# Attention block: VectorE normalises the next sample's x at step 13 of each sample instead of step 14

## The reference

```python
x = _ln(src) * (1.0 + scale) + shift          # scale, shift from the timestep of the sample
q, k, v = (heads(x @ W + b) for W, b in ...)  # 16 heads of 16 features
scores = q @ k.T / 4 + attention_bias         # bias: 8 x 16 x 512 x 512, fp32
scores = where(src_mask, -inf, scores)
ctx = softmax(scores) @ v
x = x + (ctx @ Wo + bo)
return x + gelu2(_ln(x) * g2 + beta2 @ W1 + b1) @ W2 + b2
```

## Time and profile before

| | us |
|---|---|
| median of 3 runs | 982.52 |
| lowest, highest | 981.4, 982.77 |
| the profiled execution, its own time | 980.44 |
| its span, first to last instruction | 978.6 |
| attention part: samples 1 to 8 | up to about 650 |

### The profile page before, as it was taken

How to read it: one execution, slowest core, us unless ns; L and a number is a source line. 1 busy time by engine, 2 the same in 40 slices (tenths; PEclk the granted TensorE clock), 3 DMA queues, 4 the chain that set the end, 5 groups by cost and what they waited for, 6 DMA issues and landing times. The chain is left out here.

```text
span 978.6 us, 19957 instructions
## 1 busy us (share of the span) xinstructions
PE 926.8 (95%) x5758; PEld 614.0 (63%) x5838; DVE 737.4 (75%) x1991; ACT 670.3 (68%) x1118; POOL 708.5 (72%) x568
## 2 busy tenths in 40 slices
PE   5889999999999999999999999979899999999996
PEld 5656556656656655665665665545476777777574
DVE  8886887878879788788986978788345675668465
ACT  3576978898788787889878878878544453544333
POOL 1789789788878878978896897876454455558465
PEclk9999999999999999999999999999999999999998
DMA  8988988996997899799789889965211110111101
GB/s 301 337 312 280 375 326 273 341 392 228 329 390 288 288 379 349 247 341 390 248 310 391 291 290 373 367 228 172 84 44 44 44 44 24 42 66 44 44 22 65
DMA packets 127533, 229.96 MB, mean 235 GB/s; under 512 B 6512, under 2 KB 53872, under 8 KB 123632
## 3 DMA queue, kind: packets, MB, share of 16 engines
q1 hardware_dynamic: 127472, 229.26, 65.8%
HBM read 187.30 MB, written 41.94 MB: 234 GB/s over the span
## 5 line engine op out<-in xcount | busy, mean ns | idle before, releaser
L937 ACT ACTIVATE prob<-prob,nmax 128x512 f32<-128x512 f32 x512 | 357.9, 729 | 65.7 <-DVE nmax L760 62.5
L760 DVE CUSTOM_DVE_ANT_0 prob<-s_bank,big 128x512 f32<-128x512 f32 x512 | 339.0, 686 | 74.0 <-POOL big L1111 39.0
L591 PEld LDWEIGHTS t_bank<-ident,prob 128*128 128x128 f32 x2048 | 239.0, 141 | 163.7 <-issue 48.2
L591 PE MATMUL t_bank<-ident,prob 128*128 128x128 f32 x2048 | 317.0, 277 | 16.1 <-ACT prob L937 6.0
L1111 POOL TENSOR_TENSOR big<-big,mterm_early 128x2048 f32<-128x2048 f32 (+2 forms) x78 | 271.0, 3489 | 50.2 <-DMA big<-in_fside_Bx16xSxS 34.1
L944 ACT COPY pt<-t_bank 128x512 f32<-128x512 f32 x312 | 182.0, 587 | 42.4 <-PE t_bank L591 41.2
L579 PE MATMUL s_bank<-stack_k,stack_q 128*128 128x512 bf16 x432 | 165.1, 382 | 1.3 <-DVE nmax L760 0.7
L769 DVE COPY pt<-t_bank 128x512 f32<-128x512 f32 x200 | 137.5, 688 | 31.3 <-PE t_bank L591 30.9
L605 PE MATMUL o_bank<-pt,val 128*32 128x512 f32 x1024 | 123.2, 599 | 3.7 <-issue 1.0
L2209 POOL TENSOR_TENSOR gl<-big,gh 128x512 fp32r<-128x512 f32 x64 | 83.1, 1307 | 49.8 <-DVE gh L1751 49.8
L2060 ACT ACTIVATE big<-bank,late 128x512 f32<-128x512 f32 x62 | 42.6, 690 | 72.6 <-PE bank L1458 69.8
(11 more groups left out here) (248 smaller groups left out, 1460.4 us busy)
## 6 DMA issues: line engine op xcount, KB each, us to landing
big<-in_fside_Bx16xSxS SPq DMA_DIRECT2D x128, 1024.0 KB, 7.7
pieces_dram<-pieces SPq DMA_DIRECT2D x64, 384.0 KB, 6.9
stack_q<-pieces_dram SPq DMA_DIRECT2D x15, 1024.0 KB, 8.8
stack_k<-pieces_dram SPq DMA_DIRECT2D x15, 1024.0 KB, 9.9
pieces_dram<-pieces SPq DMA_DIRECT2D x32, 256.0 KB, 7.2
xin<-in_x SPq DMA_DIRECT2D x8, 512.0 KB, 8.7
x_dram<-x SPq DMA_DIRECT2D x8, 512.0 KB, 4.5
x1r<-x_dram SPq DMA_DIRECT2D x8, 512.0 KB, 4.6
```

Of the source, the lines that this page charges most:

```text
L591: last = pe.transpose(t_bank[n % 2][:, c * P:(c + 1) * P], prob[:, n % NT, c * P:(c + 1) * P], ident[:])
L760: dve.tensor_tensor_reduce(out=prob[:, n % NT, :], in0=s_bank[n % 3][:, :], in1=bias[:, h % NB, t, :], scale=-1.0, scalar=3e38, op0=ALU.ad ...
L937: act.activation(tile, tile, ACT.Exp, bias=nmax[:, n % NT:n % NT + 1], scale=-1.0).then_inc(exped.sem, 1)
```

## The change

The constant that says at which loop position VectorE normalises goes from 14 to 13. Nothing else changes: the same instructions, with the same waits, in another order on VectorE.

```diff
 HEADS_OF_LOADS = dict(x1=3, first=2, expert=4, W1=6, mask=5, store_0=7, store_1=11)
 STACK_0_AT, STACK_1_AT = (9, 10), (0, 1)
-STATISTICS_AT, DEVIATION_AT, NORMALISE_AT = 11, 12, 14
+STATISTICS_AT, DEVIATION_AT, NORMALISE_AT = 11, 12, 13
 WEIGH_AFTER = 17
```

## The result

The changed kernel takes 985.6 us (median of 22 executions) against 981.17 us before (22 executions). The ratio is 1.0039 with an interval of 1.0028 to 1.0051: 3.8 us slower (2.7 to 5.0). The forecast was +3.6 us and 986.1 us.

The account below looks back on a forecast made before the run. PE was taken to bound each sample, busy 78.80 of 80.45 us. 6 x 0.605 = 3.63 us for samples 2 to 7 plus 0 for the first, on the median 982.52, gave 986.1 us, range 982.7 to 987.4.

Parts of the forecast that it names:

- The normalise is asked for 0.6 us earlier and ends when it ended: Samples 2 to 7: GpSimd's mask addition of head 5 holds the normalise 0.91 us; it ends 1.04 us after that addition.
- The bias addition of step 16 comes behind it, 0.605 us: VectorE, samples 2 to 7: this addition, formerly free beside GpSimd's instruction, now follows the normalise and delays W half 1.
- Nothing of it is absorbed: Samples 2 to 7: the whole lateness passes into the time, 6 x 0.605 = 3.63 us, bounds 0 and 5.4 us.
- the longer wait for x: PE's wait before transposing x in samples 2 to 7 was to stay at 0.33 us.
- The new wait before that turn: PE, before the turn of step 16: a new wait of about 0.6 us, as copy 14 must first empty its bank.
- The first sample, taken as 0: First sample: normalise held to 52.47, ending at 53.51, PE's transposition 0.9 us earlier; net 0, ends -2.6 and +0.3 us.
- The case in which VectorE comes first: First sample: VectorE might get the shared ports first, delaying GpSimd's third piece and bias 16, so nothing is gained there.
- A: Rival: the 0.6 us on VectorE vanishes in PE's lead or GpSimd's next wait; 982.5 us, chance 0.11.
- B: Rival: mask addition ends before the normalise, which isn't held; PE gets x earlier, gain up to 2.9 us, 979.6; chance 0.07.
- C: Rival: mask addition ends some tenths earlier, or first sample's clock dip vanishes; +1.9 us, 984.4 us, chance 0.16.

Follow-up runs that it names:

- h5_two_13: Kernel before with GpSimd masking two of head 5's four tiles (PE adds the other two) and the normalise at position 13: 982.55 us, ratio 1.0017.
- the two probes: Kernel before plus one 128x32 VectorE instruction at position 13: a copy from SBUF 986.96 us (ratio 1.0074), a memset 981.54 us (1.0004).
- h5_two_14: Kernel before with GpSimd masking two of head 5's four tiles (PE adds the other two), the normalise staying at position 14: 982.89 us, ratio 1.0019.
- probe_memset: Kernel before plus one VectorE memset of a 128x32 tile at position 13, the normalise staying at 14: 981.54 us, ratio 1.0004.
- the delay: Kernel before plus three VectorE statistics of a constant tile between the normalise and W half 1, some 0.6 us a sample: 983.51 us, ratio 1.0026.

## Why the prediction was right, step by step

**The normalise is asked for 0.6 us earlier and ends when it ended.** Right, and shown: the distance from GpSimd's end is 1.04 us in all six samples of the changed kernel (1.05 and 1.03 where the rounded rows are subtracted). That GpSimd is the cause and not a coincidence of the trace is shown by h5_two_13 and by the two probes. The Trainium skill says so of the forms ("SBUF — State Buffer", section "Who interferes with whom": a tensor_scalar in a two-port mode contends with GpSimd, an instruction with at most one SBUF input outside these modes doesn't). The runs agree as far as they show: normalise and copy from SBUF are held, memset, statistics and bias addition are not; which mode an instruction ran in is in no row.

**The bias addition of step 16 comes behind it, 0.605 us.** Right: 307.74 to 308.35.

**Nothing of it is absorbed.** Right in substance: the timed price is 3.8 us, and 6 x 0.605 is 3.6. In the fourth sample PE's turn of step 16 moved by 0.47 us against PE's start on x, 0.6 forecast; the rest is in the longer wait for x, which was to stay at 0.33 and is 0.46. The new wait before that turn came, and for copy 14: the turn's weight load stood idle 0.61 us for it, 0.18 before, while the matmuls themselves stood idle 0.12 us.

The size is less sure than the near hit looks. In the profiled execution the end of the normalise falls behind by 0.65 to 1.06 us a sample from the second to the seventh, 0.88 in the mean and not 0.6, since the hold grew by more than the request moved: GpSimd's addition ended 0.99 to 1.60 us behind the request (1.24 in the mean), against 0.3 to 0.9 us behind the old one (0.50). That is 0.74 us more, where the forecast had 0.60. Its start is the landing of a load, which varied in the same way before. The forecast's time of 986.1 us owes its nearness to 985.6 also to luck: it was counted from the median of three executions, 982.52, and the kernel before came to 981.17 over 22, while the medians' difference came out 0.8 us above 3.6.

**The first sample, taken as 0.** It did not go as worked out. VectorE's first two instructions of the normalise, and GpSimd's second and third piece:

```profile
51.44 1.10 DVE L798 TENSOR_SCALAR xin<-xin,mv,rstd 128x256 f32<-128x256 f32 x1
52.47 1.24 DVE L798 TENSOR_SCALAR xin<-xin,mv,rstd 128x256 f32<-128x256 f32 x1
...
51.23 1.16 POOL L1108 TENSOR_TENSOR big<-big,mterm_early 128x512 f32<-128x512 f32 x1
52.35 1.20 POOL L1108 TENSOR_TENSOR big<-big,mterm_early 128x512 f32<-128x512 f32 x1
```

I had forecast one hold, by the third piece, and the end at 53.51. But the pieces lay 1 us later than before, because their load did (a wait of 5.58 us against 4.56; the first piece starts at 50.11 and not at 49.08, ahead of everything that the change touches), so that the request met the second piece. It was held twice: the first instruction got through at the border of two pieces, the next waited out the third piece. It ended at 54.27, PE began on x at 54.40 (before, 54.55), and the 3.4 us of granted clock 0.50 behind it stayed. The case in which VectorE comes first did not arise: both times GpSimd's piece had begun 0.1 to 0.2 us before. At the end of the second sample's normalise the changed kernel is 0.97 us behind. This 1 us is in the profiled execution's 5.7 us, of which 4.4 are from there to the seventh sample, and need not be in the median's. Whether the late load makes a whole execution longer is open. Two experiments in which nothing is held anew have spans 6.0 us apart (h5_two_14 983.8 us, probe_memset 977.8 us) where their medians are 1.4 apart, and their first pieces start at 49.00 and at 47.97; but the kernel before has its first piece at 49.08 and a span of 978.6 us. So the first sample's term of 0 is neither confirmed nor refuted by the timed runs.

**The rivals.** A (absorbed) fell with the timing of the change, whose interval begins at 2.7 us; the delay points the same way and would not have sufficed alone. B (not held, PE gets x earlier and gains) did not come about, and h5_two_13 shows that it would have brought little had it done: 0.3 us less than h5_two_14 in the medians, where B reckoned with up to 2.9. C (half of it, +1.9 us) lies below that interval too, and the first sample's low clock, which it had vanish, stayed.

## What to carry to other kernels

An engine's wait for x says who is late, not that moving x's producer ahead will help: look at what the producer would run beside at the new place. An in-place fp32 tensor_scalar of VectorE belongs into a stretch in which GpSimd waits, here the 2 us before W half 1; instructions that were not held here, such as the bias addition with its PSUM input, the statistics and the memset, can fill the time of GpSimd's long ones. The sign of a hold in a trace is an instruction whose maximum is far over its median and whose end keeps a fixed distance from another engine's.

## What had not been expected

- Between two GpSimd instructions that follow each other without a gap, one held VectorE instruction gets through, and the next is held again: 1.14, 4.13 and 0.78 us in a row for what takes 0.40 alone.
- A 128x32 instruction is held to GpSimd's end like a 128x256 one: the median over the seven samples was 1103 ns and the maximum 1693; only the first, asked for when GpSimd's piece had ended, took 169.
- Moving four instructions of 1.3 us by one place earlier cost 0.4%, one place later 4.9%.
